# One product per head for the weighted values: high and low probabilities stationary side by side, 33 value columns moving

## The reference

```python
q = proj(Q, Wq, bq); k = proj(K, Wk, bk); v = proj(V, Wv, bv)     # 16 heads of 16 columns, K = V = ctx[b], 1601 x 256
scores = jnp.einsum('bhqd,bhkd->bhqk', q, k) / jnp.sqrt(jnp.float32(D_K))
attn = jax.nn.softmax(scores, axis=-1)                            # over 1601 keys
ctx = jnp.einsum('bhqk,bhkd->bhqd', attn, v)                      # the weighted values
return ctx.transpose(0, 2, 1, 3).reshape(B, S, H * D_K) @ Wo.T + bo
```

## Time and profile before

| | |
|---|---|
| three runs | 700.39, 701.28, 702.39 us; median 701.28 us |
| profiled execution | span 699.7 us from first to last instruction, 1.6 us below that median |
| busy | PE 671.0 us, DVE 552.5, POOL 549.0, ACT 443.4 |
| from 80 to 560 us (twelve batches and more) | PE 477.1 of 480 us, POOL 423.0, DVE 381.6, ACT 322.1 |
| granted TensorE clock | full speed (2.4 GHz) in all stretches used below |

### The profile page before, as it was taken

How to read it: one execution, slowest core, us unless ns; L and a number is a source line. 1 busy time by engine, 2 the same in 40 slices (tenths; PEclk the granted TensorE clock), 3 DMA queues, 4 the chain that set the end, 5 groups by cost and what they waited for, 6 DMA issues and landing times.

```text
span 699.7 us, 21737 instructions
## 1 busy us (share of the span) xinstructions
PE 671.0 (96%) x8632; PEld 507.2 (72%) x8681; DVE 552.5 (79%) x1138; ACT 443.4 (63%) x885; POOL 549.0 (78%) x374
## 2 busy tenths in 40 slices
PE   4799999999999999999999999999999998899897
PEld 2556786877777877787778777877777786677673
DVE  4697877868888878778787868787868788888867
ACT  2446766666666666676767666767675787665830
POOL 7759999999699889798989789889788786723422
PEclk9999999999999999999999999999999999999999
DMA  8587055454445454545353645363543450000212
GB/s 309 143 213 214 27 138 162 99 155 97 150 113 155 105 164 92 160 107 165 93 165 84 178 102 159 85 187 89 169 97 104 100 164 4 2 2 9 91 69 91
DMA packets 45610, 84.20 MB, mean 120 GB/s; under 512 B 8668, under 2 KB 28420, under 8 KB 45508
## 3 DMA queue, kind: packets, MB, share of 16 engines
q1 hardware_dynamic: 43896, 80.13, 41.9%
q0 software_dynamic: 912, 2.14, 1.0%
q10 hardware_dynamic: 704, 0.55, 0.3%
HBM read 36.89 MB, written 6.55 MB: 62 GB/s over the span
## 4 chain that ended last, share of the span: by engine, by line
PE 82%; DVE 5%; DMA 5%; SPq 2%; issue 2%; POOL 2%; ACT 2%; ACTq 0%; DVEq 0%; POOLq 0%
PE ps_kv L821 17%; PE ps_kv L812 16%; PE ps_score L872 12%; PE ps_out L896 12%; PE ps_front L844 12%; PE ps_score L920 2%; SPq L502 2%; DMA kstack<-khigh 2%; PE ps_out L912 1%; DMA cbuf<-in_ctxT 1%; PE ps_kv L783 1%; DMA wq_sb<-in_wqT 1%; PE ps_front L920 1%; PE ps_front L853 1%; PE ps_kv L920 1%
## 5 line engine op out<-in xcount | busy, mean ns | idle before, releaser
L637 POOL TENSOR_TENSOR plow<-prob 128x1024 bf16<-128x1024 f32 (+1 forms) x198 | 372.1, 1898 | 58.8 <-ACT prob L1242 56.3
L1511 DVE TENSOR_REDUCE maxes<-ps_front 128x1 f32<-128x512 f32 (+1 forms) x416 | 267.1, 666 | 57.2 <-PE ps_front L844 53.9
L1242 ACT ACTIVATE prob<-ps_score 128x512 f32<-128x512 f32 (+1 forms) x416 | 236.2, 598 | 71.0 <-PE ps_score L872 61.9
L872 PE MATMUL ps_score<-qstack,kstack 98*128 98x128 bf16 (+1 forms) x1664 | 150.5, 219 | 0.8 <-ACT prob L1242 0.5
L844 PE MATMUL ps_front<-kstack,qstack 96*128 96x512 bf16 (+1 forms) x512 | 145.4, 333 | 2.7 <-DMA kstack<-khigh 1.9
L872 PEld LDWEIGHTS ps_score<-qstack,kstack 98*128 98x128 bf16 (+1 forms) x1664 | 112.1, 98 | 33.7 <-ACT prob L1242 1.9
L896 PE MATMUL ps_out<-vstack,prob 128*128 128x65 bf16 (+1 forms) x1664 | 113.6, 194 | 0.7 <-POOL plow L637 0.3
L821 PE MATMUL ps_kv<-w_hi,cbuf 128*128 128x256 bf16 (+1 forms) x402 | 109.7, 273 | 0.9 <-DVE vstack L1501 0.9
L1494 DVE SCALAR_TENSOR_TENSOR klow<-ps_kv,bcol,khigh 128x512 bf16<-128x512 f32 (+1 forms) x123 | 76.8, 629 | 42.5 <-ACT khigh L1220 42.0
L821 PE MATMUL ps_kv<-w_hi,clow 128*128 128x256 bf16 (+1 forms) x402 | 109.5, 272 | 0.0
L821 PE MATMUL ps_kv<-w_lo,cbuf 128*128 128x256 bf16 (+1 forms) x402 | 109.5, 272 | 0.0
(11 more groups left out here) (290 smaller groups left out, 858.7 us busy)
## 6 DMA issues: line engine op xcount, KB each, us to landing
kstack<-khigh SPq DMA_DIRECT2D x256, 100.1 KB, 2.2
cbuf<-in_ctxT SPq DMA_DIRECT2D x15, 1601.0 KB, 7.2
kstack<-klow SPq DMA_DIRECT2D x128, 100.1 KB, 2.2
qstack<-q_blocks SPq DMA_DIRECT2D x48, 64.0 KB, 2.3
q_blocks<-qbd SPq DMA_DIRECT2D x16, 128.0 KB, 2.0
cbuf<-in_weT SPq DMA_DIRECT2D x2, 1024.0 KB, 7.8
slot_x<-att_all SPq DMA_DIRECT2D x8, 128.0 KB, 7.1
vstack<-slot_x SPq DMA_DIRECT2D x4, 256.0 KB, 3.6
```

The lines of the kernel that those rows point to most:

```text
L637: nc.gpsimd.tensor_tensor(plow[slot][0:n, :], prob[slot][0:n, :], p_high(slot, 0, HP * P)[0:n], ALU.subtract).then_inc(plow_gps, 1)
L872: mm = nc.tensor.matmul(ps_score[0:nn, h % NSB, j * P:(j + 1) * P], kstack[par][0:98, hp, n0:n0 + nn], qstack[par][0:98, q_at(hp), :], sta ...
L1242: nc.scalar.activation(prob[slot][0:nn, e * 512:e * 512 + 512], ps_score[0:nn, h % NSB, :], ACT.Exp)\
L1511: nc.vector.reduce_max(maxes[:, hp:hp + len(unit), n], ps[:, 0:len(unit) * nn].rearrange("p (h k) -> p h k", k=nn), AX.X).then_inc(m_free, 1)
```

## The change

- `prob` has for each head two blocks of 64 float32 words. ACT's exponential fills the first block, eight heads at a time, in runs of 64. `low_prob` writes the low part into the upper halves of the second block's words, so every second bfloat16 word, instead of into `plow`, which is gone.
- `vstack` has 33 columns for each of 16 heads (16 low, 16 high, a one). The copies and subtractions that fill it write runs of 16 bfloat16 numbers at a pitch of 33, where they wrote 32 at a pitch of 66.
- `weigh` does one matmul for each head: stationary are 128 columns, 64 high and 64 low, every second word of `prob`; 33 columns move. Half a chunk is eight matmuls again, all of 33 columns. The rows 0 to 63 of `ps_out` get the high part, 64 to 127 the low one.
- At a batch's end a new step on ACT (letter D, `low_outputs`) copies the lower 64 rows to the upper partitions, and DVE adds them to `ps_out`, takes 16 inverses, multiplies 64 x 512 and makes one sum instead of two.
- The weights of the second part are loaded in two pieces: the value third at once, the other two thirds later into `att_all` (fold 0 on POOL, after a wait for `w_rdy`), and the selection matrix `pick` is read with a step of zero instead of being spread out.
- All four orders are written anew.

```diff
-VW = 66
-OW = 65
+VW = 33
+OW = 33
 PE_PROGRAM = [
-    ("KKKKKKKKKKKKKmmKmmKmKmKmmKmKmKmmKmKmmmKKmmKmKmmKmKmmKKmmKmKmmsKmsmsKmsmsKmwsmswmwsKsmswmwwmKmsswmKwm"
+    ("KKKKKKKKKKKKmmKmmKmKmKmKmKmKmKmmKmKmmKmKmmKmKmmKmKmKmKmmKmKmmsKmssmKmssmKmssmwwmsKmwwsmwsmKmwssmwwmK"
...
-        prob = [sb(f"prob{p}", [P, HP * P]) for p in range(NPAR)]
-        plow = [sb(f"plow{p}", [P, HP * P], bf16) for p in range(NPAR)]
+        prob = [sb(f"prob{p}", [P, HEADS, 2, SQ]) for p in range(NPAR)]
+        prob_flat = [a[:, :, :, :].rearrange("p h r q -> p (h r q)") for a in prob]
...
-        def p_high(slot, c0, n):
-            return prob[slot][:, :].bitcast(bf16)[:, 2 * c0 + 1:2 * (c0 + n):2]
+        def p_parts(slot, part):
+            return prob_flat[slot].bitcast(bf16)[:, 1::2].rearrange("p (h r q) -> p h r q", h=HEADS, r=2)[:, :, part, :]
+        def p_columns(slot, h):
+            return prob_flat[slot].bitcast(bf16)[:, 4 * SQ * h + 1:4 * SQ * (h + 1):2]
...
-            pool.dma_start(wqkv_sb[:, :, :], wqkv.rearrange("(k p) n -> p k n", p=P)).then_inc(ld_t, 16)
+            pool.dma_start(wv2_sb[:, :, :], wqkv.rearrange("(k p) n -> p k n", p=P)[:, :, 2 * D:3 * D]).then_inc(ld_t, 16)
...
                     pool.wait_ge(wrot_rdy, 2)
+                    pool.wait_ge(w_rdy, 3)
+                    pool.dma_start(wqk_raw, wqkv.rearrange("(k p) n -> p k n", p=P)[:, :, 0:2 * D]).then_inc(ld_t, 16)
...
             def low_prob(b, k):
-                nc.gpsimd.tensor_tensor(plow[slot][0:n, :], prob[slot][0:n, :], p_high(slot, 0, HP * P)[0:n],
+                nc.gpsimd.tensor_tensor(p_parts(slot, 1)[0:n], prob[slot][0:n, :, 0, :], p_parts(slot, 0)[0:n],
                                         ALU.subtract).then_inc(plow_gps, 1)
...
-                for part in range(2):
-                    for hp in range(4 * half, 4 * half + 4):
-                        o = ps_out[:, half, (hp % 4) * OW:(hp % 4 + 1) * OW]
-                        lhs = plow[slot][0:nn, hp * P:(hp + 1) * P] if part else p_high(slot, hp * P, P)[0:nn]
-                        mm = nc.tensor.matmul(o[:, 32 * part:OW], lhs, vstack[par][0:nn, k, hp, 32 * part:OW],
-                                              start=(k == 0 and part == 0 and hp % 4 == 0),
-                                              stop=(k == NCH - 1 and part == 1 and hp % 4 == 3),
-                                              skip_group_check=True)
+                for h in range(HP):
+                    mm = nc.tensor.matmul(ps_out[:, half, h * OW:(h + 1) * OW], p_columns(slot, HP * half + h)[0:nn],
+                                          vstack[par][0:nn, k, HP * half + h, :],
+                                          start=(k == 0 and h == 0), stop=(k == NCH - 1 and h == HP - 1),
+                                          skip_group_check=True)
...
-                nc.scalar.activation(prob[slot][0:nn, e * 512:e * 512 + 512], ps_score[0:nn, h % NSB, :], ACT.Exp)\
+                nc.scalar.activation(prob[slot][0:nn, HP * e:HP * e + HP, 0, :],
+                                     ps_score[0:nn, h % NSB, :].rearrange("p (h q) -> p h q", h=HP), ACT.Exp)\
                     .then_inc(exp_done, 1)
...
+            def low_outputs(b):
+                act.wait_ge(pv_done, NCH * (b + 1))
+                wait(act, out_read, b)
+                wait(act, att_done, b)
+                nc.scalar.copy(oparts[:, :, :, :], ps_out[SQ:2 * SQ, :, 0:HP * OW].rearrange("p a (h c) -> p a h c", c=OW))\
+                    .then_inc(out_low, 1)
...
             def divided(b):
-                dve.wait_ge(pv_done, NCH * (b + 1))
-                rows = ps_out[:, :, 0:4 * OW].rearrange("p a (h c) -> p a h c", c=OW)
-                nc.vector.reciprocal(orec[:, :, :], rows[:, :, :, 64]).then_inc(out_inverse, 1)
+                dve.wait_ge(out_low, b + 1)
+                rows = ps_out[0:SQ, :, 0:HP * OW].rearrange("p a (h c) -> p a h c", c=OW)
+                nc.vector.tensor_tensor(rows, rows, oparts[:, :, :, :], ALU.add).then_inc(out_sums, 1)
+                dve.wait_ge(out_sums, b + 1)
+                nc.vector.reciprocal(orec[:, :, :], rows[:, :, :, 2 * DH]).then_inc(out_inverse, 1)
```

More of the change, by code:

```diff
@@ L345, in build @@
         pT = [a.rearrange("p (h n) -> p h n", h=HP) for a in kbd_flat]
-        late_rooms += [prob[n][:, :] for n in range(3)]
+        late_rooms += [prob_flat[n][:, 0:HP * P] for n in range(3)]
         late_used += [0, 0, 0]
@@ L922, in product3 @@
                 for i, (cols, row, bias) in enumerate(biases):
-                    mm = nc.tensor.matmul(dst[:, cols], pick[:, row, :], high(bias), start=False,
+                    mm = nc.tensor.matmul(dst[:, cols], pick[:, row:row + 1].to_broadcast([SEL, P]), high(bias), start=False,
                                           stop=(i == len(biases) - 1), skip_group_check=True)
@@ L1058, in counts @@
                 a, b = GROUPS[g]
-                pe.wait_ge(ones_set, 3)
+                pe.wait_ge(ones_set, 4)
                 pe.wait_ge(ev["mask"], g + 1)
@@ L1081, in experts @@
                          lambda k: we_low[k][:, cols],
-                         [(slice(a * D, (a + 1) * D), 2 * pair + a, bias3[:, 2 * D:3 * D]) for a in range(2)])\
+                         [(slice(a * D, (a + 1) * D), 2 * pair + a, bias3[:, :]) for a in range(2)])\
                     .then_inc(ev["e_ps"], 1)
@@ L1193, in first_values @@
                 nc.scalar.copy(v0_stage(u)[0:rows, 0:nch * D], kv_bank(0, u)[0:rows, 0:nch * D]).then_inc(v0_rdy, 1)
[L1194 to L1195 removed]
+                nc.scalar.copy(vstack[0][0:rows, c0:c0 + nch, :, DH:2 * DH],
+                               kv_bank(0, u)[0:rows, 0:nch * D].rearrange("p (c h d) -> p c h d", c=nch, h=HEADS))                    .then_inc(kv_free_act, 1)
             def query_high(t):
@@ L1227, in high_part @@
                         wait(act, pv_done, NCH * (b - 1))
-                    nc.scalar.copy(vstack[par][0:rows, c0:c0 + nch, :, 32:64],
-                                   kv_bank(b, u)[0:rows, 0:nch * D].rearrange("p (c h d) -> p c h d", c=nch, h=HP))\
+                    nc.scalar.copy(vstack[par][0:rows, c0:c0 + nch, :, DH:2 * DH],
+                                   kv_bank(b, u)[0:rows, 0:nch * D].rearrange("p (c h d) -> p c h d", c=nch, h=HEADS))\
                         .then_inc(high_done, 1)
@@ L1327, in _ @@
             shifts = iter([(b, half) for b in BATCHES for half in range(2)])
-            query_tiles = iter(range(TILES))
+            query_tiles, outputs = iter(range(TILES)), iter(BATCHES)
             tiles = {kind: iter(range(TILES)) for kind in "AHVTB2fi"}
@@ L1347, in _ @@
                     copy_shift(*next(shifts))
+                if letter == "D":
+                    low_outputs(next(outputs))
                 if letter == "Z":
@@ L1543, in attended @@
                     dve.wait_ge(zeros_sent, 16 * (E + BY_SLOT))
-                col = b // 2 * D
-                parts = oparts[:, :, :, :].rearrange("p a h (q j d) -> p (a h) j d q", q=2, j=2)
-                for j in range(2):
-                    dst = att_all[64 * (b % 2):64 * (b % 2) + 64, col:col + D].rearrange("p (h j d) -> p h j d", h=HP, j=2)
-                    nc.vector.reduce_sum(dst[:, :, j, :], parts[64 * j:64 * j + 64, :, j, :, :], AX.X).then_inc(att_done, 1)
+                dst = att_all[SQ * (b % 2):SQ * (b % 2) + SQ, b // 2 * D:b // 2 * D + D]
+                nc.vector.reduce_sum(dst.rearrange("p (h d) -> p h d", h=HEADS),
+                                     oscaled.rearrange("p a h (r d) -> p (a h) d r", r=2), AX.X).then_inc(att_done, 1)
             def constants():
```

151 lines of the change are left out of this document (77 added, 74 removed).

## The result

The changed kernel takes 707.01 us (median of six runs, 703.76 to 710.92), the kernel before, beside it, 701.92 us (six runs, 700.39 to 702.57). The ratio is 1.0074, with a 95% interval of 1.0046 to 1.0102: slower by 0.7%. Forecast were 692.2 us, in a range of 687.5 to 703.5. The profiled execution of after took 707.28 us, with a span of 705.5 us; the span before was 699.7 us.

What follows compares the result with a forecast made beforehand. PE was taken as the bound, busy 477.1 of 480 us from 80 to 560 us. 699.7 - 10.7 - 0.7 + 0.5 + 0.8 + 1.0 = 690.6 us span, plus 1.6 gives 692.2 us; range 687.5 to 703.5.

Steps and rivals of the forecast that it cites:

- the sum: Forecast of the whole span: 699.7 - 10.7 - 0.7 + 0.5 + 0.8 + 1.0 = 690.6 us.
- Eight matmuls at 25 ns: Weighing on PE: each 33-column matmul keeps 25 ns, 0.03 us less a half; 10.7 us in the long window, 0.7 later.
- the first rival: Weighing: the gapped matrix's load sets the pace; 715.6 us at 33 ns, 703.6 at 29 ns; chance 0.07 each.
- `low_prob` on POOL: Low part of probabilities: runs and gapped writes cost 87 ns each, hidden from 80 to 560 us, +0.5 us before.
- the second rival: POOL becomes the bound through `low_prob`, 80 to 560 us: 730 us at a quarter more, 788 at 42%; chance 0.07.
- The end of batch 14: Gap between weighings on PE grows from 2.02 to 2.8 us, with ACT's copy between exponentials: +0.8 us.
- The other fourteen ends: Remaining batch ends: some 2.5 us of PE work covers the longer chain; 1.0 us for all, at worst 5.6 us.
- the third rival: Longer chain at batch ends shows: 0.4 us for each of 15, 696.4 us; with twice that 702 us; chance 0.14.
- The new orders: Engine orders: only the first batch's new order was priced, at nothing, within +-1 us shared with a later transfer.
- The rest: Exponentials and values in runs hidden on ACT and DVE; later POOL transfer and first batch's new order nothing, +-1 us.
- The statement on PE's idle time: Sign of a wrong prediction: PE's idle time between 80 and 560 us, 2.9 us before, grows beyond 8.

Runs made afterwards that it cites:

- the run with the old tail: The changed kernel, its new orders kept up to about 560 us and the previous kernel's orders from there on: 703.8 us, ratio 1.0014 to 1.0048.
- the kernel with the copies at later places: New product, old orders, DVE's sum before a multiplication on POOL; ACT's copy one to four letters later in eight batches: 701.0 us against 699.3 us.

## Why the prediction was wrong

The 14.8 us between 692.2 and 707.0 us can be laid out along three runs, in the order product, end, new orders: 695.0 for 701.5 (-6.5, where the sum had -10.9 with `low_prob`), then 703.7 (+8.7, where it had +1.8), then 707.0 (+3.3, where it had nothing). So 4.4, 6.9 and 3.3 us were missed in these terms; the other 0.2 us are the kernel before, 701.5 beside these runs. The split is one of several, since the parts are not independent: in the new orders the end costs 2.9 us, 1.1 more than the sum had, and without the end the new orders cost 704.1 - 695.0 = 9.1 us.

By place, in us of each trace, cut at the first weighing of batch 0, the first of batch 14 and the start of the last weighing:

| kernel | ahead of the first weighing | batches 0 to 13 | batches 14 and 15 | behind | span |
|---|---|---|---|---|---|
| before | 64.0 | 487.8 | 53.1 | 94.8 | 699.7 |
| after | 67.5 | 485.2 | 54.4 | 98.4 | 705.5 |
| new product, old orders | 64.6 | 487.0 | 55.9 | 94.8 | 702.3 |
| old product, new orders | 67.1 | 489.5 | 53.3 | 99.8 | 709.7 |
| after without the batch's end | 67.0 | 482.6 | 53.7 | 98.3 | 701.6 |
| new product, old orders, without it | 64.8 | 479.1 | 54.2 | 94.9 | 693.0 |

After loses 3.5 us ahead of the first weighing and 3.6 behind the last, where the sum had 0.5 and nothing. In batches 0 to 13 it gains 2.6 us, where the sum had some 10.

**Eight matmuls at 25 ns: the price right, what arrives of it too large.** 48 matmuls of 33 columns start at 153.29 us, and what follows them at 154.50: 1.21 / 48 = 25 ns, with the gapped matrix under all of them, as the earlier trace rows let expect. It is the timeline of PE after:

```profile
153.29 1.37 PE L906 MATMUL ps_out<-vstack,prob 128*128 128x33 bf16 x48
154.50 0.41 PE L866 MATMUL ps_front<-ident_bf,mwords 128*98 128x128 bf16 x4
```

So the first rival falls, at both of its prices. But only 6.5 us of the 11.4 us of the sum arrive at the end, even with the old orders and no longer end. There batches 0 to 13 are 8.7 us shorter, with waits up from 2.0 to 4.5 us in the long window; of these 4.5, some 1.3 us stand before weighings that wait for `low_prob`, 1.2 before scores that wait for exponentials and 1.2 before maxima that wait for transfers. The first weighing comes 0.8 us later, and batches 14 and 15 take 1.1 us more, where the sum had 0.7 less. The sum put all these waits at nothing; why batches 14 and 15 grew was not tried.

**`low_prob` on POOL: right in kind, too dear.** From 80 to 560 us it takes 1,898 ns, where the earlier trace rows have 1,893 and the sum had 1,980. Reading in runs and writing every second word cost 5 ns in place of 87. POOL is busy 425.7 of 480 us: the second rival falls too.

```profile
L650 POOL TENSOR_TENSOR prob<-prob 128x1024 bf16<-128x1024 f32 x167 | 313.6, 1898 | 35.8 <-ACT prob L1252 34.9 <-PE ps_out L906 0.2
```

**The end of batch 14: right, and one thing more.** The sum had +0.8 us. After, PE and then ACT:

```profile
575.39 0.76 PE L906 MATMUL ps_out<-vstack,prob 128*128 128x33 bf16 x24
576.00 0.68 PE L885 MATMUL ps_score<-qstack,kstack 98*128 98x128 bf16 x8
577.52 0.40 PE L885 MATMUL ps_score<-qstack,kstack 98*128 98x128 bf16 x4 [0.84 <-ACT prob L1252]
578.29 0.89 PE L885 MATMUL ps_score<-qstack,kstack 98*128 98x128 bf16 x8 [0.37 <-ACT prob L1252]
579.16 0.38 PE L906 MATMUL ps_out<-vstack,prob 128*128 128x33 bf16 x8
```

```profile
576.25 0.60 ACT L1268 COPY oparts<-ps_out 64x528 f32<-64x528 f32 x1
576.87 0.60 ACT L1252 ACTIVATE prob<-ps_score 128x512 f32<-128x512 f32 x1
```

The last weighing ends before 576.00 us, the next starts at 579.16: 3.16 us, against 2.02 us in the earlier trace rows, so +1.1 us, with the copy between the exponentials as described. What the prediction left out came behind it: the granted clock.

**The other fourteen ends: this step failed.** The sum had 1.0 us for all, 5.6 us at worst, from the 2.5 us of PE work between the weighings. It looked only at the release of the next weighing. In the old orders the end costs 8.7 us, 0.54 us for each of the 16, a price between the two of the third rival, which had a chance of 0.14. The first weighing of a batch is only a small part of that: of the 12.0 us of waits in the old orders, by starts, 1.9 us stand before weighings that wait for `oparts` and 4.5 before maxima that wait for DVE's. DVE stands in the end for 0.6 us more and waits for ACT's copy first, and behind it stand the maxima, for which PE waits. The prediction named this queue ("behind DVE's sum, row maxima and low parts") and then priced it at nothing by the idle time of a whole window (98 us on DVE). An average over 480 us says nothing of a pause of 0.6 us at a place where PE comes for the result. In the new orders the end costs less, 2.9 us, and PE's waits on DVE are nearly gone: there the larger miss is in the orders themselves.

**The new orders: this step failed.** "The rest" had nothing with 1 us either way for the new order. With the old product the new orders cost 9.4 us; in the traces, 3.1 us ahead of the first weighing, 1.9 up to the last and 5.0 behind it. There was no rival by which the four strings cost time by themselves; that they are new was read for two places only. Two stretches can be named. One is the second part, 3.2 us by the run with the old tail. The other is the beginning: all five runs with the new order there have their first weighing at 67.0 to 71.7 us, all others at 63.2 to 66.1. Among the runs whose granted clock stayed at 1.00 from 16 us to there, it is 67.0 and 67.5 against 63.2 to 64.8. Which part of the new beginning costs this was not tried by itself.

The largest single wait of after, 2.32 us in batch 3, looks like a third place, but isn't one of the order alone. SP, and then PE after:

```profile
153.26 2.50 SPq L505 DMA_DIRECT2D qstack<-q_blocks  x3
155.81 0.52 SPq L512 DMA_DIRECT2D kstack<-khigh  x1
```

```profile
158.32 0.36 PE L906 MATMUL ps_out<-vstack,prob 65*128 65x33 bf16 x8
161.00 0.59 PE L857 MATMUL ps_front<-kstack,qstack 96*128 96x512 bf16 x2 [2.32 <-DMA kstack<-khigh]
```

SP issues the queries' transfers for 2.5 us, those of `kstack` follow from 155.81 us on, and PE, there at 158.5 us, waits for them. After without the batch's end waits 2.4 us there as well; the run with the old tail, whose order up to 560 us is the same, waits 0.3 us, as the kernel before does.

**The statement on PE's idle time was no guard.** It was to rise above 8 us if the prediction was wrong; it rose from 2.9 to 5.2 us, and the time was 5 us worse all the same. Waits counted by starts, 2.0 and 9.9 us, would have shown it.

What stays open: why copy and sum together cost 2.7 us more than each for itself; why the kernel with the copies at later places is slower; which exchange in the second part's new order costs its 3 to 4 us; and which one in the beginning costs its 2 to 4 us. In the profiled execution of after the first transfer of `x_all` landed 4.6 us after its issue, before 3.5 us; up to 1.1 us of the later start may come from this, and not from the order.

## What to carry to other kernels

When a hand-made order keeps one engine 99% busy, a new step on another engine is not hidden by that engine's free time in the mean: ask what stands behind it in its queue at that place, and who comes for it. An order that was made anew is a change of its own, with a price of its own; run the old product with the new order and the new product with the old one, before the sum of both is explained. And count waits of a pipelined engine from start to start, since its busy time covers them.
